# Two eviction products of a token-mixing stage moved off VectorE for halves 2 to 5

## The reference

```python
x = x + attn(_layernorm(x))          # token mixing by a decaying scan
x = x + ffn(_layernorm(x))           # six nodes of full attention
# attn:
x = layernorm(x) * ln_g + ln_b;  last_x = x shifted by one token
k = (x*mix_k + last_x*(1-mix_k)) @ Wk.T   # v, r alike
den = den*td + exp(k);  num = num*td + exp(k)*v      # scan over the 1024 tokens
out = sigmoid(r) * num/(den + 1e-8) @ Wo.T
# ffn: for c in range(6):
q, k, v = ew[c,:] * (nodes[...] @ We[...] + be[...])
nodes[c] = act_w[c] * mha(q, k, v, Wq[c], Wk[c], Wv[c], Wo[c]) + q   # 8 heads, 1024 keys
out = layernorm(nodes[5]) * fln_g + fln_b
```

## Time and profile before

| | |
|---|---|
| median of 3 runs | 2249.14 us (2245.19 to 2252.85) |
| the profiled execution's own time | 2245.28 us |
| its span in the profile | 2243.5 us |
| busy share of the span | PE 97%, DVE 92%, ACT 80%, POOL 24% |
| mean granted clock of TensorE | 0.994 of full speed |
| instructions | 43662 |

### The profile page before, as it was taken

One profiled execution on the slowest core, in us unless ns is written; L12 is line 12 of the kernel. 1 busy time (PEld: TensorE's weight loads), 2 busy tenths in 40 slices (PEclk: granted clock), 3 DMA queues, 4 the chain that ended last, 5 costly groups with the idle time before them and its releaser, 6 DMA issues.

```text
span 2243.5 us, 43662 instructions
## 1 busy us (share of the span) xinstructions
PE 2182.0 (97%) x16565; PEld 885.5 (39%) x16565; DVE 2064.3 (92%) x3252; ACT 1796.7 (80%) x3432; POOL 530.1 (24%) x667
## 2 busy tenths in 40 slices
PE   7999999999999999999999999999999999999997
PEld 3533333343333443443433433433433434434332
DVE  6999999999989999999999999999999999999895
ACT  4377887888778888888888888888888888788776
POOL 4431221312203113123023022022121121431213
PEclk9999999999999999999999999999999999999999
DMA  4230422414223134133232242242242242241301
GB/s 127 65 75 22 83 55 67 81 45 85 60 59 80 50 72 82 53 81 73 54 79 65 58 83 58 56 93 55 59 84 55 57 85 54 59 99 43 75 25 53
DMA packets 87536, 149.39 MB, mean 67 GB/s; under 512 B 35146, under 2 KB 49950, under 8 KB 87326
## 3 DMA queue, kind: packets, MB, share of 16 engines
q0 software_dynamic: 28224, 94.13, 20.0%
q1 hardware_dynamic: 59102, 52.46, 9.4%
HBM read 42.36 MB, written 14.91 MB: 26 GB/s over the span
## 4 chain that ended last, share of the span: by engine, by line
PE 76%; DVE 11%; SPq 7%; DMA 4%; issue 2%; ACT 1%; POOL 0%; POOLq 0%; DVEq 0%; ACTq 0%
PE context L660 28%; PE ring L615 26%; PE wide L639 8%; DVE max_neg L1279 4%; SPq L1593 4%; DVE max_neg L1276 3%; PE wide L550 2%; PE wide L530 2%; PE wide L522 2%; DMA q_aug<-rows_dram 2%; DMA rows_dram<-max_turn 2%; PE wide L555 2%; SPq L1590 1%; PE wide L541 1%; PE context L485 1%
## 5 line engine op out<-in xcount | busy, mean ns | idle before, releaser
L906 ACT ACTIVATE e_ring<-ring 128x512 f32<-128x512 f32 x3053 | 1603.7, 602 | 302.6 <-PE ring L615 300.5
L1276 DVE TENSOR_REDUCE max_neg<-wide 128x1 f32<-128x512 f32 x1800 | 1132.7, 682 | 87.6 <-PE wide L639 84.5
L639 PE MATMUL wide<-k_aug,q_aug 48*128 48x512 f32 x3072 | 1057.3, 440 | 14.0 <-DVE max_neg L1279 6.7
L615 PE MATMUL ring<-q_aug,k_aug 50*128 50x512 f32 x3053 | 1042.6, 437 | 16.1 <-DMA q_aug<-rows_dram 15.2
L660 PE MATMUL context<-e_ring,v_aug 128*32 128x256 f32 (+1 forms) x9240 | 905.0, 463 | 1.0 <-ACT raw L915 0.9
L1279 DVE TENSOR_REDUCE max_neg<-wide 128x2 f32<-128x1024 f32 x636 | 771.8, 1218 | 26.3 <-PE wide L639 20.2
L615 PEld LDWEIGHTS ring<-q_aug,k_aug 50*128 50x128 f32 x3053 | 492.7, 185 | 726.0 <-ACT e_ring L906 608.5
L639 PEld LDWEIGHTS wide<-k_aug,q_aug 48*128 48x128 f32 x3072 | 500.2, 185 | 40.2 <-DVE max_neg L1279 15.8
L660 PEld LDWEIGHTS context<-e_ring,v_aug 128*32 128x32 f32 x9240 | 184.7, 108 | 412.1 <-issue 293.3
L395 POOL DMA_DIRECT2D src<-node_dram x40 | 22.9, 572 | 672.8 <-DMA rows_dram<-max_turn 672.8
L1381 POOL CAST q_part<-q_part 128x512 fp32r<-128x512 f32 x46 | 28.1, 611 | 397.5 <-DVE max_turn L1298 214.2
(11 more groups left out here) (245 smaller groups left out, 938.7 us busy)
## 6 DMA issues: line engine op xcount, KB each, us to landing
q_aug<-q_part POOLq DMA_DIRECT2D x138, 256.0 KB, 4.3
k_aug<-k_part POOLq DMA_DIRECT2D x138, 256.0 KB, 6.5
src<-node_dram POOLq DMA_DIRECT2D x40, 512.0 KB, 7.2
ctxT<-raw SPq DMA_DIRECT2D x380, 32.0 KB, 2.0
rden_bc<-rden_dram SPq DMA_DIRECT2D x23, 512.0 KB
node_dram<-node_ring SPq DMA_DIRECT2D x16, 512.0 KB, 2.7
q_aug<-rows_dram SPq DMA_DIRECT2D x192, 8.0 KB
node_ring<-in_L_attn_x SPq DMA_DIRECT2D x4, 512.0 KB, 5.3
```

The lines of the kernel that those rows point to most:

```text
L615: e.matmul(bk[:, :], k_aug[first:first + AUG, u % 2, h // 2, chunk * P:(chunk + 1) * P].bitcast(F32R), q_aug[first:first + AUG, u % 2, h / ...
L639: e.matmul(bk[:, :], q_aug[first:first + SPLIT, u % 2, head // 2, q0:q0 + P].bitcast(F32R), k_aug[first:first + SPLIT, u % 2, head // 2, h ...
L906: e.activation(e_ring[:, n % E_SLOTS, :], bank[where["st", n]][:, :], ACT.Exp, scale=EXP_SCALE).then_inc(a_exp, 1)
L1276: e.tensor_reduce(max_neg[:, G % 2, kh, row:row + 1], wide[:, b, :], AX_X, ALU.max, negate=True).then_inc(v_mx, 1)
```

## The change

For halves 2 to 5 (`SHARED_OUT`) the two DVE instructions go. At `PROJ_V` ACT copies the values out of PSUM into `ekv`, and POOL multiplies `ekv` by `ek` in place. At `OUT` PE first multiplies `xs` by the identity into the bank and then accumulates the four products with Wo on it, and ACT copies the bank to `xs`. Semaphores `a_v`, `g_ekv` and `a_x2` take the place of `v_ekv` and `v_x2` for these halves; the bank of the values is freed by the ACT copy. The times in `MIX_AT` stay.

```diff
--- before.py
+++ after.py
@@ -166,6 +166,7 @@
         d_rden_out, d_rden_in, d_last_den = sems("d_rden_out d_rden_in d_last_den")
         d_bias_out, d_bias_in = sems("d_bias_out d_bias_in")
         p_last_den, g_w_last, g_to_values, d_w_last, v_x2b = sems("p_last_den g_w_last g_to_values d_w_last v_x2b")
+        a_v, a_x2, g_ekv = sems("a_v a_x2 g_ekv")
         d_x, d_x2_out, d_spill = ([sem(f"{n}{b}") for b in range(B)] for n in ("d_x", "d_x2_out", "d_spill"))
         d_q0, d_k0 = ([sem(f"{n}{i}") for i in range(PAIRS)] for n in ("d_q0_", "d_k0_"))
         d_rows, d_max_in, d_ctx, d_den, d_x2_last, d_ones = (
@@ -223,6 +224,7 @@
          INV_D, GATE, OUT, STAT2, INVERSE2, APPLY2, TURN2) = range(24)
 
         LERPED = (6, 7)
+        SHARED_OUT = (2, 3, 4, 5)
         COLUMNS_AT = 2
         EDGE_TURNS = -(-3 * NODES // 4)
 
@@ -270,6 +272,18 @@
             if u + 1 < LAST:
                 return (22, 25), (23, 26), (24, 27), 28, 31
             return (20, 22), (21, 23), (22, 24), 25, 28
+
+        def residual_added(i):
+
+            if i in SHARED_OUT:
+                return a_x2, SHARED_OUT.index(i) + 1
+            return v_x2, 1 + i - sum(j < i for j in SHARED_OUT)
+
+        def values_weighted(i):
+
+            if i in SHARED_OUT:
+                return g_ekv, SHARED_OUT.index(i) + 1
+            return v_ekv, 1 + i - sum(j < i for j in SHARED_OUT)
 
         def mix_stages(time):
             return [(i, k) for i in range(2 * B) for k, at in enumerate(MIX_AT[i]) if at == time]
@@ -452,7 +466,9 @@
                         e.wait_ge(a_xT, i + 1)
                         e.matmul(bk[:, :], w_time_t[:, 2 * n, :], xT[:, 1:BANK + 1], start=True, stop=False)
                         e.matmul(bk[:, :], w_time_t[:, 2 * n + 1, :], xT[:, 0:BANK], start=False, stop=True).then_inc(signal, 1)
-                    freed[at] = ((a_ek, v_ekv, a_er)[n], i + 1)
+                    freed[at] = ((a_ek, i + 1), values_weighted(i), (a_er, i + 1))[n]
+                    if k == PROJ_V and i in SHARED_OUT:
+                        freed[at] = (a_v, SHARED_OUT.index(i) + 1)
                 if k == OUT:
                     at = where["out", i] = pick()
                     bk = free_bank(at)
@@ -460,11 +476,15 @@
                         e.wait_ge(v_gate, i + 1)
                     else:
                         e.wait_ge(g_gate, i + 1 - EARLY)
+                    if i in SHARED_OUT:
+                        e.wait_ge(d_x[i // 2], DMA)
+                        e.matmul(bk[:, :], ident[:, :], xs_of(i), start=True, stop=False)
                     for j in range(CPB):
                         done = e.matmul(bk[:, j * P:(j + 1) * P], ekv[:, j * P:(j + 1) * P], w_time_t[:, 6, :],
-                                        start=True, stop=True)
+                                        start=i not in SHARED_OUT,
+                                        stop=i not in SHARED_OUT or j == CPB - 1)
                     done.then_inc(p_mo, 1)
-                    freed[at] = (v_x2, i + 1)
+                    freed[at] = residual_added(i)
                 if k == TURN2:
                     if i < EARLY:
                         e.wait_ge(v_n2, i + 1)
@@ -796,6 +816,12 @@
                 if k == PROJ_K:
                     e.wait_ge(p_mk, i + 1)
                     e.activation(ek, bank[where["k", i]][:, :], ACT.Exp).then_inc(a_ek, 1)
+                if k == PROJ_V and i in SHARED_OUT:
+                    e.wait_ge(p_mv, i + 1)
+                    e.activation(ekv, bank[where["v", i]][:, :], ACT.Copy).then_inc(a_v, 1)
+                if k == OUT and i in SHARED_OUT:
+                    e.wait_ge(p_mo, i + 1)
+                    e.activation(xs_of(i), bank[where["out", i]][:, :], ACT.Copy).then_inc(a_x2, 1)
                 if k == PROJ_R:
                     e.wait_ge(p_mr, i + 1)
                     e.activation(er, bank[where["r", i]][:, :], ACT.Exp, scale=-1.0).then_inc(a_er, 1)
@@ -1056,7 +1082,7 @@
                     e.wait_ge(v_lerp, 4 * LERPED.index(i) + 1)
                     e.scalar_tensor_tensor(out=(ek, ekv, er)[n], in0=y, scalar=col[:, C_MIX + n:C_MIX + n + 1], in1=xT[:, 0:BANK],
                                            op0=ALU.mult, op1=ALU.add).then_inc(v_lerp, 1)
-                if k == PROJ_V:
+                if k == PROJ_V and i not in SHARED_OUT:
                     e.wait_ge(p_mv, i + 1)
                     e.wait_ge(a_ek, i + 1)
                     e.tensor_tensor(ekv, bank[where["v", i]][:, :], ek, ALU.mult).then_inc(v_ekv, 1)
@@ -1070,7 +1096,7 @@
                         e.wait_ge(v_den, i + 1)
                         step(e.tensor_copy(keep[0], y[:, BANK - 1:BANK]))
                 if k == NUM:
-                    e.wait_ge(v_ekv, i + 1)
+                    e.wait_ge(*values_weighted(i))
                     done = e.tensor_tensor_scan(num, td, ekv, 0.0 if hf == 0 else keep[1], ALU.mult, ALU.add)
                     step(done)
                     if hf == 0:
@@ -1091,11 +1117,11 @@
                     e.wait_ge(v_inv, 4 * i + 4)
                     after()
                     e.tensor_tensor(ekv, num, ek, ALU.mult).then_inc(v_gate, 1)
-                if k == OUT:
+                if k == OUT and i not in SHARED_OUT:
                     e.wait_ge(p_mo, i + 1)
                     e.tensor_tensor(xs, bank[where["out", i]][:, :], xs, ALU.add).then_inc(v_x2, 1)
                 if k == STAT2:
-                    e.wait_ge(v_x2, i + 1)
+                    e.wait_ge(*residual_added(i))
                     statistics(xs, i)
                 if k == INVERSE2:
                     inverse(i, (1.0, LN_EPS), v_var2)
@@ -1355,6 +1381,11 @@
 
             def mix(i, k):
                 y, ek, ekv, er, num = mixing_sets[i]
+                if k == PROJ_V and i in SHARED_OUT:
+                    e.wait_ge(a_ek, i + 1)
+                    e.wait_ge(a_v, SHARED_OUT.index(i) + 1)
+                    after()
+                    signal(e.tensor_tensor(ekv, ekv, ek, ALU.mult), g_ekv)
                 if k == INVERSE:
                     e.wait_ge(v_var, i + 1)
                     power(i, g_rs1)
```

## The result

The changed kernel takes **2255.37 us** (median of 20 runs, 2245.79 to 2277.82) and the kernel before 2248.45 us (20 runs, 2235.42 to 2255.34): ratio **1.0041, 95% interval 1.0023 to 1.006**. The forecast was 2253.6 us, 0.2% slower; the range of 2248.0 to 2260.0 holds the result. The forecast's ratio, 2253.6 / 2249.14 = 1.0020, lies just under the first interval and inside the second.

The account below looks back on a forecast made before the run. It took PE to decide in steps -12 to -1 and 176 to 200 us, DVE from 140.5 to 176, an engine relay in the prologue. 2.6 + 1.7 - 0.2 - 0.4 + 0.8 = +4.5 us gave 2253.6 us, range 2248.0 to 2260.0.

Parts of the forecast that it names:

- Values of half 2: Prologue: POOL's new multiplication stands ahead of half 3's normalisation and half 1's power, delaying the first maxima by 2.6 us.
- the clock falls in the new gap: Rival, prologue: PE's 4.2 us idle gap lowers the clock, costing 1.7 us more, total +6.2 us (2255.3); chance 0.27.
- a low clock between 45 and 52 us: Prologue: a low granted clock at these times, named as a sign that the forecast is wrong.
- the low clock lasts through the relay: Rival, prologue: low clock over PE's 5 to 5.5 us of work after 46 us, total +10 us (2259.1); chance 0.13.
- Values of half 3: Turn 29: POOL's multiplication fits behind its twelve transfers, where POOL idled; cost 0, bounds 0 and +0.5 us.
- `OUT` of halves 2 and 3: Steps -12 and -7, where PE decides: two identity products lie on the path, +1.7 us.
- Values of halves 4 and 5: Steps 2 and 8: ACT frees the bank earlier for PE; -0.2 us for both, bounds -0.5 and +0.6.
- `OUT` of half 4: Step 12, where DVE decides: its sum goes, PE takes part back; -0.4 us, bounds -0.7 and +0.2.
- `OUT` of half 5: Step 22, where PE decides: +0.8 us, bounds 0 and +0.9.
- that test of the prediction: After the edited stretches: lag about 4.5 us at 200 us that stays; growth after 211 us would show the forecast wrong.
- DVE everywhere: Rival, whole kernel: DVE decides everywhere, so all 5.5 us are gained, perhaps -7 us (2242); chance 0.04.
- the relay has slack: Rival, prologue: transfers or ACT end last before the first maxima, so the 2.6 us goes; +1.9 us (2251.0); chance 0.14.

Follow-up runs that it names:

- e4: The changed kernel with four unread 512-column products added on PE ahead of its wait for half 3's normalisation; ratio 1.0026 to the kernel before.
- e5: The whole change, but POOL multiplies half 2's values between its normalisation of half 3 and its power of half 1; ratio 1.0014 to the kernel before.
- e2: The kernel before with only the values of halves 2 to 5 moved, in the change's queue place, residuals left on DVE; ratio 0.9993.
- e8: The changed kernel measured again, unaltered, on another chip; ratio 1.0026 to the kernel before.
- e9: A repeat of e6 in other rounds; median 2239.91 us, ratio 0.9983 to the kernel before.
- e7: The kernel before with only the residuals of halves 2 and 3 moved to PE and ACT, no values; ratio 1.0016.
- e3: The kernel before with only the residuals of halves 2 to 5 moved to PE and ACT, values left on DVE; ratio 1.0017.
- e10: The kernel before with only the values of halves 2 to 5 moved, half 2's multiplication behind half 3's normalisation; median 2242.69 us, ratio 0.9976.
- e11: The kernel before with only the residual of half 4 moved to PE and ACT, no values; ratio 1.0004.
- e6: The kernel before with values of halves 2 to 5 moved, half 2's multiplication behind half 3's normalisation, and half 4's residual alone; 2242.24 us, ratio 0.9981.
- e12: As e6, with the residual of half 5 moved to PE and ACT as well; ratio 0.9993 to the kernel before.
- e1: The changed kernel with POOL's multiplication for half 2 moved behind its power of half 1; median 2252.99 us, ratio 1.003 to the kernel before.

## Why the prediction was right, and where it was not

*Values of half 2, +2.6 us: right.* The relay lost 2.69 us with the clock kept high (e4). Its steps came out one by one: multiplication at 40.0 (40.04 without the later start), normalisation 4.46 (4.45), power about 1.0 (1.03), DVE's normalisation 2.58 us later (47.90 - 0.75 - 44.42 = 2.73). The first maxima stand at 61.93 in e4, which started 0.43 us late, so 61.5, where the prediction has 61.4. And e5 confirms it from the other side: in POOL's idle 3.16 us the same instruction costs 0.07. With the clock low, the path behind the normalisation was PE's (51.27 to 52.77, the last product ahead of the transposes), not DVE's, which ended at 49.01. With it high (e4) the two are equal, as the prediction had them: DVE ends at 48.70, and that product starts at 48.76.

*The rival "the clock falls in the new gap", given 0.27: this is what happened*, in all three profiles with that gap (changed, e2, e8), and in none of the others. It is also what the prediction had named as a sign of being wrong, a low clock between 45 and 52 us. The prediction put its price at 1.7 us, by the fall at 177 us, and it measured 2.68. The low level lasted 6.8 us (twice the 3.4 us that the windows lack to 1.00), where that at 177 us lasted 3.4. This is past the 2.2 us of loss from which, by the prediction, the other clock rival decides ("the low clock lasts through the relay", given 0.13). Its price of 5 to 5.5 us was not reached: PE's head products at 53.89 and 54.86 ran at full clock. The step that failed is the choice between forecast and rival: the gap of 4.2 us was foreseen, and was held to be too little by "the fully used 128-row products around it". The row that should have weighed more was the fall after 1.86 us in the earlier trace rows: more than twice that gap could hardly be the safer case. The rule quoted from the Trainium skill ("TensorE: Matmul & The Clock Gate", "HAM oscillation — how this bites in real kernels"), that long waits of PE put it back to the low clock, was right here. With its price at 2.7 the rival gives 2256.3, and the result is 2255.37. The forecast lies 1.8 us under the result. Against the kernel before, whose median came out 0.7 us lower than in the three runs, it is 2.5 us short (+4.5 against +6.9), near the 2.68 us that it lacks. That these agree so well is in part luck: on the other chip the medians differ by 3.7 us.

*Values of half 3, 0: nearly.* All kernels with shared values and a high clock take 0.2 to 0.3 us less from the first maxima to step 0 (42.03 to 42.09 against 42.29). DVE starts its first maximum 1.1 us behind PE's (e9: 59.78 and 58.64) instead of 1.4 (60.17 and 58.81), which the prediction did not look at. No run has half 3's values alone, so that the difference belongs to them is not shown.

*`OUT` of halves 2 and 3, +1.7: right* (1.68 in e7, 1.69 in e3, 1.72 between e10 and e5).

*Values of halves 4 and 5, -0.2, and `OUT` of half 4, -0.4:* from step 0 to the eviction at 162.50 the change gains 0.34 us (the lag goes from 12.07 to 11.73; in e8 from 7.73 to 7.39), e10 0.10 and e11 0.25. Two more profiles agree: e2, with the values as in e10, gains 0.11 there, and e3, with the residual of half 4 and not the values, 0.23. Both signs right, both about half as large. They do not quite add up: e6 and e9, which have both, gain 0.22 and 0.23.

*`OUT` of half 5, +0.8: right* (0.84).

Sum of the terms as measured: 2.69 - 0.26 + 1.7 - 0.34 + 0.84 = +4.6, with 2.68 for the clock +7.3. Time x clock, which leaves the clock out, has +4.8 for the changed kernel and +3.9 for e8. The medians differ by 6.9 us on the first chip; over the 32 runs of the changed kernel and the 105 of before the means (2255.4 and 2247.0) differ by 8.4. The lag does not stay at 4.5 after 211 us, but moves with each later fall of the clock, as it does for kernels that change nothing there; that test of the prediction could not decide anything.

*"DVE everywhere", 0.04, and "the relay has slack", 0.14:* both false in the profiles: the first maxima move with the relay in the changed kernel and back with it in e5, and PE's products cost their full time in e7 and e12.

**What stays open.** The 2.68 us of clock in the relay are in the profiles, but no total shows them: e2 has the same fall and the time of before, and e4, without the fall, is not faster than e8. The four kernels that share the values and not the residuals of halves 2 and 3, 5 (e2, e6, e9, e10: 48 runs) have a mean clock of 0.9936, before has 0.9922, and the kernels with residuals of halves 2 and 3 have 0.9903 to 0.9927. Some 3 us of the gain of e6, e9 and e10 are this. In their profiles the fall near 620 us is missing, which before, the changed kernel (twice), e7 and e11 show; but e1, e3, e4, e5 and e12 lack it too, and e2 has its high mean in spite of the fall at 47 us. Summed over windows of 2 us, the profile lacks 15.3 us of full clock before, 9.2 in e6 and 8.5 in e9 (which also lack the falls near 345 and 2180), but 16.5 in e10. Whether the program or its timing by some microseconds decides which falls occur, these runs don't tell.

## What to carry to other kernels

An instruction moved to an idle engine costs what it delays in that engine's queue: look for the idle slot that ends latest before the next critical instruction, and for a neighbour on DVE that wants the same port. Here the move of the values gained only in the right slot (0.9976, and most of that gain is not explained), and the residuals of halves 2, 3 and 5 cost PE, which had no slack, the full 0.84 us each. And a new wait of PE can have two prices, the wait and the clock behind it. Products into a free bank while it waits saved the second, 2.7 us, in the profile, though not visibly in the total.

## What was not expected of the hardware

- The granted clock fell to 0.50 with PE busy all 2.00 us of each window before and during it, at 93 us in one profile of the changed kernel and at 85 us in e12, but not in e8 and the others. It cost about 4.5 us (48.26 against 43.75 in e8, and 46.53 against 42.09 in e9). The Trainium skill, "TensorE: Matmul & The Clock Gate", section "A second HAM failure mode: psum-queue depth-cycling", tells of falls where PE pauses briefly and often between groups; the records show no pause here.
- The same gap does not always bring the fall, and the length of a gap alone does not decide. All 14 profiles have the wait of 1.84 to 1.86 us that stands before 175.99 us in the kernel before. In 13 the clock falls behind it. In e8 the wait comes 7.4 us later, as all else does, and the windows stay at 1.00. Yet the longer wait of 2.49 us in e1's prologue brought no fall.

```profile
183.37 0.50 PE L659 MATMUL wide<-k_aug,q_aug 48*128 48x512 f32 x1 [1.86 <-DVE max_neg L1305]
```
```profile
184.00:186.00 2.00, 2.00 (x17) 1.42 (x20) 2.00 (x3) 0.82 (x2) 0.00 (x0) 1.00 0.01 4
186.00:188.00 2.00, 2.00 (x20) 0.46 (x12) 1.73 (x3) 1.49 (x4) 0.00 (x0) 1.00 0.01 4
```

- The low stretch behind that wait lasted 3.4 us in eight of the 13 profiles, 6.8 us in four and 13.7 us in one (e5), by twice what the windows of 2 us lack to 1.00.
